# A fused attention and expert kernel: per-item input products as two row tiles side by side, and two output additions set at another place among the rotations

## The reference

```
c   = einsum('bct,bcd->bdt', x, w[subject[b]]) + bias[subject[b]]   # 64x64 weights, one of 8 per item
x   = x + attention(c)      # 16 heads, 64 tokens per item, latents of 128, rotations, causal softmax, WZ, bZ
x   = x + ffn(cond2(x))     # a linear layer with adapters, then 4 experts, each on 1024 of the 4096 tokens
```

## Time and profile before

| | |
|---|---|
| median of three runs | 1913.26 us |
| the profiled execution's own time | 1914.91 us |
| its span, first to last instruction | 1912.7 us |
| TensorE matmuls (PE) | 1820.7 us busy, 95% |
| TensorE weight loads (PEld) | 1417.9 us, 74% |
| VectorE (DVE) | 925.2 us, 48% |
| GpSimd (POOL) | 703.3 us, 37% |
| ScalarE (ACT) | 630.4 us, 33% |
| mean granted TensorE clock | 0.985 |

### The profile page before, as it was taken

One profiled execution on the slowest core, in us unless ns is written; L12 is line 12 of the kernel. 1 busy time (PEld: TensorE's weight loads), 2 busy tenths in 40 slices (PEclk: granted clock), 3 DMA queues, 4 the chain that ended last, 5 costly groups with the idle time before them and its releaser, 6 DMA issues. The chain is left out here.

```text
span 1912.7 us, 29404 instructions
## 1 busy us (share of the span) xinstructions
PE 1820.7 (95%) x10664; PEld 1417.9 (74%) x10664; DVE 925.2 (48%) x1581; ACT 630.4 (33%) x1088; POOL 703.3 (37%) x525
## 2 busy tenths in 40 slices
PE   6799999999999999999999997999999999999996
PEld 4577776767777676777687776888888888888884
DVE  4565667566666656656423783242423333333321
ACT  4333333333333333333223112333333333333331
POOL 1231322123132212313000034565657575757563
PEclk9999999999999999999999998999999999999998
DMA  7000101010010201002132115033304220522001
GB/s 261 23 1 17 52 6 62 7 61 2 17 51 6 62 7 62 1 17 62 37 106 105 61 61 191 19 88 110 66 0 110 99 55 0 132 88 44 9 13 22
DMA packets 68587, 104.80 MB, mean 55 GB/s; under 512 B 12304, under 2 KB 29456, under 8 KB 68496
## 3 DMA queue, kind: packets, MB, share of 16 engines
q1 hardware_dynamic: 53568, 76.92, 12.1%
q0 software_dynamic: 7200, 16.78, 4.8%
q10 hardware_dynamic: 7728, 9.71, 1.4%
HBM read 78.23 MB, written 25.17 MB: 54 GB/s over the span
## 5 line engine op out<-in xcount | busy, mean ns | idle before, releaser
L1858 DVE CAST hh<-hid 128x512 fp32r<-128x512 f32 x128 | 92.5, 723 | 453.1 <-ACT hid L1803 453.1
L1728 POOL TENSOR_TENSOR w1l<-w_raw,w1h 128x512 fp32r<-128x512 f32 x112 | 185.1, 1653 | 153.3 <-ACT w1h L1795 153.2
L441 POOL TENSOR_TENSOR prob<-prob,rinv 128x512 f32<-128x512 f32 x64 | 70.4, 1100 | 465.4 <-DVE rinv L700 465.4
L95 PE MATMUL bank_o<-Mh,mix_h 128*128 128x512 f32 x512 | 211.4, 413 | 20.5 <-DVE x_res L707 19.1
L95 PE MATMUL e_h<-xh,w1h 128*128 (+1 forms) x512 | 203.5, 397 | 5.6 <-POOL w1l L1728 5.6
L96 PE MATMUL e_h<-xl,w1h 128*128 (+1 forms) x512 | 202.6, 396 | 0.0
L97 PE MATMUL e_h<-xh,w1l 128*128 (+1 forms) x512 | 202.5, 395 | 0.0
L97 PE MATMUL bank_o<-Mh,mix_l 128*128 128x512 f32 x512 | 202.1, 395 | 0.0
L96 PE MATMUL bank_o<-Ml,mix_h 128*128 128x512 f32 x512 | 201.7, 394 | 0.0
L95 PE MATMUL e_y<-w2h,hh 128*128 128x512 f32 x512 | 201.2, 393 | 0.0
L96 PE MATMUL e_y<-w2l,hh 128*128 128x512 f32 x512 | 200.6, 392 | 0.0
(11 more groups left out here) (303 smaller groups left out, 3486.9 us busy)
## 6 DMA issues: line engine op xcount, KB each, us to landing
w_raw<-in_W_dram SPq DMA_DIRECT2D x56, 512.0 KB, 4.5
stage<-in_x_dram SPq DMA_DIRECT2D x8, 1024.0 KB, 5.8
x_res<-in_x_dram SPq DMA_DIRECT2D x32, 256.0 KB, 3.5
out_dram<-x_res SPq DMA_DIRECT2D x32, 256.0 KB, 2.0
flat_dram<-flat_sb ACTq DMA_DIRECT2D x32, 256.0 KB, 2.0
rows<-out_dram SPq DMA_DIRECT2D x4, 1024.0 KB, 5.3
stage<-in_W_dram SPq DMA_DIRECT2D x8, 512.0 KB, 5.4
x_res<-out_dram SPq DMA_DIRECT2D x3, 1024.0 KB, 5.1
```

Of the source, the lines that this page charges most:

```text
L95: nc.tensor.matmul(out, ah, bh, start=start and n == 0, stop=False)
L441: nc.gpsimd.tensor_tensor(prob[:, i % 2, :, :], prob[:, i % 2, :, :], rinv[:, :].unsqueeze(2).to_broadcast([P, HB, C]), ALU.mult).then_inc ...
L1728: nc.gpsimd.tensor_tensor(w1l[:, k, :, :], w1_at(pair, chunk), w1h[:, k, :, :].bitcast(F32), ALU.subtract).then_inc(S["w1_lo"], 1)
L1858: nc.vector.tensor_copy(hh[:, k, :], hid[:, k, :]).then_inc(S["h_hi"], 1)
```

## The change

Each item's product becomes a matmul of its own on its 64 rows, so no zeros are multiplied: the loaded operand is 64 rows by 128 columns, the moving one 64 by 64, and the item's parity in the pair picks the bank. Four calls of `cond` with four matmuls each become two calls (`half`) with sixteen each; each half fills both banks, each bank with two chunks. So `lb_ev` is waited for before the first half, and the second half waits for both evictions of the first. The evictions `cond_hi` and `cond_lo` stay four each, now for one parity of two chunks, through the strided view `cond_half`. ScalarE and VectorE do two evictions ahead of the last softmax step of the group, where it was one. TensorE does three heads of `wz` between the halves and five behind them. On VectorE `x2_tile(g, 0)` goes ahead of rotation 7, and `x2_tile(g, 5)` goes behind rotation 2.

```
-                for n in range(NPAIR):
-                    last = nc.tensor.matmul(bank_p[(c + 1) % 2][:, n * P:(n + 1) * P], x_cond[:, n, c * P:(c + 1) * P],
-                                            K["wblk"][:, n, :], start=True, stop=True)
-                last.then_inc(S["cond_mm"], 1)
+                last = {}
+                for c in range(2):
+                    for n in range(NPAIR):
+                        for j in range(2):
+                            rows = slice(j * C, (j + 1) * C)
+                            cols = slice((2 * half + c) * P, (2 * half + c + 1) * P)
+                            last[j] = nc.tensor.matmul(bank_p[j][:, (c * NPAIR + n) * C:(c * NPAIR + n + 1) * C],
+                                                       x_cond[rows, n, cols], K["wblk"][rows, n, 0:C],
+                                                       start=True, stop=True)
+                last[0].then_inc(S["cond_mm"], 1)
+                last[1].then_inc(S["cond_mm"], 1)
...
                     cond(g + 1, 0)
-                    wz(g, 4, (0, ))
+                    wz(g, 4, (0, 1, 2))
                     cond(g + 1, 1)
-                    wz(g, 4, (1, 2))
-                    cond(g + 1, 2)
-                    wz(g, 4, (3, 4))
-                    cond(g + 1, 3)
-                    wz(g, 4, (5, 6, 7))
+                    wz(g, 4, (3, 4, 5, 6, 7))
...
+            def cond_hi(g, k):
+                act.wait_ge(S["cond_mm"], g * TC + k // 2 * 2 + 2)
+                nc.scalar.copy(cond_half(cond_h, k), bank_p[k % 2][:, :].rearrange("p (c n d) -> p c n d", c=2, n=NPAIR)
+                               ).then_inc(S["cond_hi"], 1)
...
                 queries_rope(g, 6)
+                x2_tile(g, 0)
                 queries_rope(g, 7)
-                x2_tile(g, 0)
...
                     keys_rope(g + 1)
-                    queries_rope(g + 1, 0)
-                    queries_rope(g + 1, 1)
+                    for u in range(UB - 1):
+                        queries_rope(g + 1, u)
                 x2_tile(g, 5)
                 if more:
-                    queries_rope(g + 1, 2)
-                    queries_rope(g + 1, 3)
+                    queries_rope(g + 1, UB - 1)
                     less_max(g + 1, 0)
```

More of the change, by code:

```diff
@@ L106, in spread_weights @@
         s = dve.value_load(K["subj"][0:1, bass.ds(g * GB + j, 1)], min_val=0, max_val=NSUB - 1)
-        nc.vector.tensor_copy(K["wblk"][rows, n, rows], K["wsub"][rows, bass.ds(s, 1), :].squeeze(1)
+        nc.vector.tensor_copy(K["wblk"][rows, n, 0:C], K["wsub"][rows, bass.ds(s, 1), :].squeeze(1)
                               ).then_inc(K.sems["wblk_ready"], 1)
@@ L374, in attention, with cond_half @@
         NR = NU + 1
+        def cond_half(tile, k):
+            view = tile[:, :, :].rearrange("p c (n j d) -> p c n j d", n=NPAIR, j=2)
+            return view[:, k // 2 * 2:k // 2 * 2 + 2, :, k % 2, :]
         def over_groups(eng, first, body):
@@ L588, in body @@
                     cond_hi(g + 1, 0)
+                    cond_hi(g + 1, 1)
                 exps(g, 7)
                 if more:
-                    for c in range(1, TC):
-                        cond_hi(g + 1, c)
+                    cond_hi(g + 1, 2)
+                    cond_hi(g + 1, 3)
                     latent_hi(g + 1, 0)
@@ L618, in _, with cond_lo @@
         def _(dve):
[L619 to L622, removed]
+            def cond_lo(g, k):
+                dve.wait_ge(S["cond_hi"], g * TC + k + 1)
+                nc.vector.tensor_tensor(cond_half(cond_l, k),
+                                        bank_p[k % 2][:, :].rearrange("p (c n d) -> p c n d", c=2, n=NPAIR),
+                                        cond_half(cond_h, k).bitcast(F32), ALU.subtract).then_inc(S["cond_lo"], 1)
             def latent(g, i):
@@ L767, in body @@
                     cond_lo(g + 1, 0)
+                    cond_lo(g + 1, 1)
                 softmax_sum(g, 7)
                 if more:
-                    for c in range(1, TC):
-                        cond_lo(g + 1, c)
+                    cond_lo(g + 1, 2)
+                    cond_lo(g + 1, 3)
                 x2_tile(g, 4)
@@ L806, in bias_rows, with cond @@
                                  start=True, stop=True).then_inc(S["bias_mm"], 1)
-            def cond(g, c, first=False):
-                if c == 0:
+            def cond(g, half, first=False):
+                if half == 0:
                     pe.wait_ge(S["x_in"], g * 16 + 16)
                     pe.wait_ge(S["wblk_ready"], g * GB + GB)
+                    pe.wait_ge(S["lb_ev"], g * 2 + 2)
                     if not first:
                         pe.wait_ge(S["ka_ev"], g * NH)
-                elif c == 1:
-                    pe.wait_ge(S["lb_ev"], g * 2 + 2)
-                else:
-                    pe.wait_ge(S["cond_lo"], g * TC + c - 1)
-                for n in range(NPAIR):
-                    last = nc.tensor.matmul(bank_p[(c + 1) % 2][:, n * P:(n + 1) * P], x_cond[:, n, c * P:(c + 1) * P],
-                                            K["wblk"][:, n, :], start=True, stop=True)
-                last.then_inc(S["cond_mm"], 1)
+                else:
+                    pe.wait_ge(S["cond_lo"], g * TC + 2)
+                last = {}
[9 more added lines that the diff above has]
+                last[1].then_inc(S["cond_mm"], 1)
             def latent(g, i):
@@ L940, in first @@
                 bias_rows(0, first=True)
-                for c in range(TC):
-                    cond(0, c, first=True)
+                for half in range(2):
+                    cond(0, half, first=True)
                 latent(0, 0)
```

3 lines of the change are left out of this document (removed).

## The result

The changed kernel takes 1928.8 us (median of four runs, 1927.53 to 1929.47); the kernel before took 1912.4 us in the same comparison (1910.33 to 1914.07). The ratio is 1.0077 [1.0062, 1.0092]: 16.4 us slower. The profiled execution of the changed kernel is the shortest of its runs, that of the kernel before lies above its median, so the two spans, 1925.4 and 1912.7, are only 12.7 apart.

The account below looks back on a forecast made before the run. TensorE's order of work was taken to set the time; -7.5 + 14.8 + 2.2 + 2.0 + 10.5 = +22.0 us gave 1936.9 from the profiled execution, 1935 on the median's base, range 1919 to 1945.

Parts of the forecast that it names:

- the likeliest case: Whole kernel: all five steps together, 1935 us, with its own range of 1929 to 1942; chance 0.58.
- Step 1: Addition 0 ahead of rotation 7: TensorE's wait ahead of step 1's first head goes in eight groups, -7.5 us.
- Step 2: Addition 5 behind rotation 2: the wait ahead of step 6's first head grows in seven groups, +14.8 us.
- Step 3: Input product in the loop's groups: pairs 0.11 us apart by their loads, plus changes of tiling, +2.2 us.
- B: Input product's halves: not bound by loading, a chunk costs half, the clock still falls; 1921.5 us, chance 0.07.
- C: Input product's halves: the same halving of cost, and the clock stays up; 1911 us, chance 0.04.
- D: Input product's halves: a pair's loads run one behind the other; 1963 us, chance 0.03.
- Step 4: Group 0's input product: nothing stands between the halves, so evictions are waited for and `latent` starts later, +2.0 us.
- Step 5: Behind the longer stalls at addition 5: the clock falls in most of seven groups, 7 x 1.5 = +10.5 us.
- Rival A: Behind the longer stalls at addition 5: no fall of the clock; 1925 us, chance 0.24.

Follow-up runs that it names:

- e1_add0: The kernel before with output addition 0 alone moved ahead of rotation 7: 1910.3 us, ratio 0.9969.
- e8_four_tiles: The changed kernel with addition 5 behind rotation 0, and the input product in four 64x64 tiles with five heads between the halves: 1899.2 us, ratio 0.9919.
- e7_first_chunks: e10_add5_between with group 0's input product in four chunks as in the kernel before: 1898.1 us, ratio 0.9911.
- e9_fill: The changed kernel with fifteen idle 512-column matmuls ahead of step 6's first head, in the wait for addition 5: 1920.5 us, ratio 1.0029.
- p1_pad_first: The kernel before with 16 tiny idle matmuls, once, ahead of group 0's bias product: 1901.9 us, ratio 0.9934.
- e10_add5_between: The changed kernel with addition 5 placed inside rotation 1, between its multiplication and its addition: 1890.8 us, ratio 0.9881.

## Why the prediction came out as it did

Slower, mainly by the steps it named, and the time lies in the range given, just below the likeliest case's own. But two sizes were wrong, and a gain it had not seen, of the other sign, hides that: the closeness of the sum is in part luck.

- **Step 1**, -7.5 us: right. All eight waits are gone, and `e1_add0` has groups of 110.3 instead of 111.3.
- **Step 2**, +14.8: right in place and kind, a little too small. The wait is 3.88 in the mean of seven instead of 1.53, so 7 x 2.35 = +16.5. Rotation 2 in front takes 2.34 rather than 2.11: the 2.11 was read where the shuffle starts 0.06 before the end of the output addition, but behind rotation 1, which ends at 294.71, it starts at 294.88.
- **Step 3**, +2.2: right, 7 x 0.32. The pairs are 0.112 apart, as priced, so the halves of 1 us (rivals B and C) and of 3.5 us (D) fall. The row that the price came from the earlier trace rows is of a whole matmul behind row tiles, not of one on 64 rows; the pairs' distance confirms it for those. `e8_four_tiles` shows that the price is that of the loads.
- **Step 4**, +2.0: the term that was mis-sized. `latent` starts 14.15 us behind the bias product instead of 8.70, and the whole first group lost 7.9 us, which `e7_first_chunks` gave back. The clock was left out: it is at 0.50 from 49.3 to 66.4 us, where the kernel before shows 3.4 us of that. At 0.50 a pair takes 0.213 (3.68 for a half), and `latent` starts 3.5 later than the 10.65 behind the bias product that were priced; the 4.8 us of low clock behind `latent`'s start cost half their length, 2.4. That these two make up the 5.9 beyond the price is worked out, not tried by itself, and why the clock stays low there so long is open.
- **Step 5**, +10.5: right. The clock falls behind each of the seven stalls, for 3.4 us, and `e9_fill` puts it at 1.53 a group (112.71 less 111.19): 7 x 1.53 = +10.7. Rival A falls with it. The row that gave the price was not a clean one. The fall at 647.95 came right behind a wait at the head of the loop, which the prediction doesn't mention, and this wait was 0.53 longer than in the neighbour that the group was held against; a shorter wait for addition 0 (0.68 instead of 1.00) and one of 0.35 that was missing made up for it. The fall shows, too, that it doesn't take a stall of 3.6 us:

```profile
646.50 0.65 PE L884 MATMUL bank_s<-k_absorbed,q 128*64 128x256 f32 x3 [1.58 <-issue]
```

- **Not in the prediction**: the wait at the head of the loop. The view of waits had it, 8.3 us in six places, and the prediction doesn't mention it. The new product has 32 matmuls ahead of the loop where there were 16, and 32 a pass in it; with it the instructions are no longer fetched again, and `p1_pad_first` shows that matmuls ahead of the loop suffice for that: in the length of a group 1.83 us (109.47 in `p1_pad_first`, 111.3 before), six times, -11.0.

The sum is -7.5 + 16.5 + 2.2 + 7.9 + 10.7 - 11.0 = +18.8 in the attention. Its end moved from 953.0 to 969.5, +16.5, and its first bias product from 48.55 to 47.40, so it is 17.7 longer. The 1.1 between the two is the one group of 112.37 in the kernel before, as the terms are taken against 111.3. In the code behind the attention, which is the same, 3.8 us are missing; the clock was low for 17.1 us there, 27.3 before, and no run here tells why. So the time of 1935 came out 6 us high: the gain of 11.0 that was not seen outweighs by 3.2 the losses that were priced too low (1.7, 5.9 and 0.2), and the other 3 lie outside these terms.

## What to carry to other kernels

Before an elementwise step is moved past another, look at both engines' rows at that place: here TensorE was already waiting for the step, and of the four places tried the one that left no wait was inside a rotation, early enough for one consumer and not too early for the other. A wait put down to "issue" at the head of a loop is a cost of its own that an edit of the code ahead can bring back or take away, so a difference of a few per thousand between two kernels should be checked for it, in the waits and in the count of instruction transfers, before they are credited to the edit. When a matmul has few moving columns, count the columns that are loaded.

## What was not expected of the hardware

- A loop of some 1,550 TensorE records a pass may or may not have its instructions fetched again at each pass: 79 transfers or 25 and 26, 1.8 us a pass, changed by 16 tiny matmuls ahead of it. Which place is a good one stays open; the lengths tried don't give the rule.
- Loads of weights slow down with the clock: pairs are 0.112 us apart at 1.00 and 0.213 at 0.50.
- Matmuls whose result nobody uses, put into a stall of 3.9 us, keep the clock at 1.00 behind it and save 1.5 us. A better place for the step saves 5.6 (112.7 to 107.1 a group).
- The fall at the same stall of 3.9 us lasted 6.8 us in six groups of seven with the old product and 3.4 with the new one; why stays open.
- A wait of 1.58 us at the head of the loop had a fall of the clock behind it once (646.50), and one of 1.67 (201.4) had none; which it will be, no run here tells.

A kernel with `e10_add5_between`'s order, a cheaper product in group 0, and a loop that isn't fetched again was not run; by the figures here it would be near 1883 us, an estimate (1890.8 less 7.9).
